# Projection units that hold half heads: two chunks a batch instead of four, and two groups of stacks read at the batch's head

## What is computed

```python
xn  = layernorm(x)
qkv = xn @ qkv_w + qkv_b                       # 512 -> 3 x 512, 32 heads of width D = 16
x1, x2 = split(q or k, 2, axis=-1)             # lower and upper 8 of a head's 16
q or k = concat([x1*cos - x2*sin, x2*cos + x1*sin])
ctx = softmax(causal(q @ k.T / sqrt(16))) @ v  # 32 heads, 512 x 512 scores
x = x + (ctx @ out_w + out_b) * silu(swiglu_ffn(xn))
x = x + block1_attn(layernorm(x)) * silu(block1_ffn(layernorm(x)))
```

## Time and profile before

| quantity | value |
|---|---|
| median of 3 runs | 650.18 us (648.63 to 650.63) |
| profiled execution, its own time | 646.0 us |
| span of the profile | 644.1 us |
| PE / DVE / ACT / POOL busy | 605.6 / 381.3 / 276.1 / 377.7 us |
| mean granted TensorE clock | 0.999 |
| batch 0: PE starts its first unit, slot 0 | 15.12, 40.07 us |
| batch 1: PE starts its first unit, slot 0 | 235.22, 259.79 us |

### The profile page before, as it was taken

The page is one execution under the profiler, slowest core; times in us unless marked ns, Lnnn a source line. Parts: engine busy times, 40 slices in busy tenths (PEclk is TensorE's granted clock), DMA queues, the critical chain, the costliest instruction groups (busy, mean ns, idle before and its releaser), DMA issues.

```text
span 644.1 us, 9815 instructions
## 1 busy us (share of the span) xinstructions
PE 605.6 (94%) x3348; PEld 417.9 (65%) x3348; DVE 381.3 (59%) x918; ACT 276.1 (43%) x439; POOL 377.7 (59%) x596
## 2 busy tenths in 40 slices
PE   2997999999999999889999999999999999999996
PEld 2865565666557888555556665687887566757564
DVE  4958768666426495786775663466975261515275
ACT  3524555555643633255554556355122343222323
POOL 4876656555334578676565553447989474921254
PEclk9999999999999999999999999999999999999999
DMA  8778865753422327568477644824600000000012
GB/s 284 221 224 280 248 177 146 209 135 92 98 99 67 99 82 214 171 187 243 134 220 226 177 104 117 319 81 172 204 26 1 0 1 2 0 1 0 2 50 82
DMA packets 60225, 83.63 MB, mean 130 GB/s; under 512 B 17920, under 2 KB 26496, under 8 KB 60176
## 3 DMA queue, kind: packets, MB, share of 16 engines
q1 hardware_dynamic: 57392, 73.84, 38.9%
q10 hardware_dynamic: 2784, 9.18, 4.0%
HBM read 65.17 MB, written 26.99 MB: 143 GB/s over the span
## 4 chain that ended last, share of the span: by engine, by line
PE 75%; DVE 8%; POOL 5%; DMA 5%; issue 3%; SPq 2%; ACT 2%; DVEq 0%; ACTq 0%; POOLq 0%
PE proj_ps L922 9%; PE ctx_ps L1080 6%; PE proj_ps L923 6%; PE proj_ps L924 6%; PE score_ps L952 5%; PE proj_ps L1128 3%; PE scoreT_ps L961 3%; PE score_ps L922 3%; PE proj_ps L1129 3%; PE score_ps L924 2%; PE score_ps L923 2%; PE scoreT_ps L922 2%; PE scoreT_ps L924 2%; PE scoreT_ps L923 2%; POOL w_lo L741 2%
## 5 line engine op out<-in xcount | busy, mean ns | idle before, releaser
L741 POOL TENSOR_TENSOR w_lo<-raw,w_hi 128x512 fp32r<-128x512 f32 x98 | 132.7, 1359 | 67.8 <-ACT w_hi L1272 61.2
L1447 DVE CUSTOM_DVE_ANT_0 score_ps<-score_ps,causal 128x512 f32<-128x512 f32 (+3 forms) x256 | 120.0, 517 | 58.0 <-PE score_ps L952 57.6
L1316 ACT ACTIVATE probs_T<-scoreT_ps 128x1024 f32<-128x1024 f32 (+1 forms) x96 | 84.9, 884 | 80.9 <-PE scoreT_ps L961 80.1
L922 PE MATMUL proj_ps<-xn_hi,w_hi 128*128 128x512 f32 x224 | 99.5, 444 | 0.3 <-POOL w_lo L741 0.3
L923 PE MATMUL proj_ps<-xn_hi,w_lo 128*128 128x512 f32 x224 | 88.1, 393 | 0.0
L924 PE MATMUL proj_ps<-xn_lo,w_hi 128*128 128x512 f32 x224 | 87.8, 392 | 0.0
L739 POOL TENSOR_SCALAR w_hi<-raw 128x512 fp32r<-128x512 f32 x50 | 31.2, 625 | 49.4 <-PE proj_ps L924 48.5
L897 POOL TENSOR_TENSOR hsL<-hidden_T,hsH 128x256 fp32r<-128x256 f32 x44 | 38.2, 884 | 36.1 <-ACT hsH L1399 35.8
L922 PEld LDWEIGHTS proj_ps<-xn_hi,w_hi 128*128 128x128 f32 x224 | 41.9, 187 | 24.5 <-issue 9.5
L775 POOL TENSOR_SCALAR_AFFINE_SELECT probs_T<-probs_T 128x256 f32<-128x256 f32 x128 | 50.6, 416 | 10.9 <-ACT probs_T L1316 10.9
L952 PE MATMUL score_ps<-k_st,q_st 50*128 50x512 f32 (+3 forms) x256 | 44.4, 383 | 13.0 <-DVE row_max L1447 8.8
(11 more groups left out here) (303 smaller groups left out, 1307.9 us busy)
## 6 DMA issues: line engine op xcount, KB each, us to landing
raw<-w SPq DMA_DIRECT2D x98, 256.0 KB, 2.8
rows<-rows_hi SPq DMA_DIRECT2D x32, 256.0 KB, 3.8
arranged<-tern SPq DMA_DIRECT2D x96, 85.0 KB
q_st<-rows SPq DMA_DIRECT2D x32, 200.0 KB
k_st<-rows SPq DMA_DIRECT2D x32, 200.0 KB
rows<-rows_lo SPq DMA_DIRECT2D x16, 256.0 KB, 4.4
gate_w<-arranged ACTq DMA_DIRECT2D x4, 704.0 KB, 7.0
up_w<-arranged ACTq DMA_DIRECT2D x4, 704.0 KB, 7.8
```

The source lines that it names most:

```text
L741: nc.gpsimd.tensor_tensor(w_lo[n % SPLIT][:, :], raw[n % RAW][:, :], F32(w_hi[n % SPLIT][:, :]), ALU.subtract).then_inc(unit_ready, 1)
L922: nc.tensor.matmul(acc, lh, rh, start=first, stop=False)
L1316: nc.scalar.activation(probs_T[gp % 4][:, c:c + 2 * w].rearrange("p (h c) -> p h c", h=2), scoreT_ps[:, :, 0:w], ACT.Exp, scale=0.25).then ...
L1447: m = nc.vector.tensor_tensor_reduce(out=block, in0=block, in1=causal[:, S - w:], scale=1.0, scalar=-3e38, op0=ALU.add, op1=ALU.max, accum ...
```

## The change

A query or key unit now holds only the lower or only the upper 8 dimensions of 16 heads, so there are two chunks of 16 heads a batch, of four units each: query lower, query upper, key lower, key upper (`QK_UNIT`). `rope_first` needs two instructions of 128 partitions, `by_cos` and `by_sin`, and `rope_second` combines the cosine part of one half with the sine part of the other: lower = cos(lower) - sin(upper), upper = cos(upper) + sin(lower). So the sum of either half waits until both halves have been projected (`upper`, `turned_in`). The doubled tiles are now one for lower and one for upper.

The first chunk's four units stand at the head: FILL = 8, V is units 4 to 7, and two units (8 and 9) are run before slot 0 instead of three; 96 triples instead of 100 are dealt to the 53 slots. The second chunk's are units 9, 11, 13 and 15. `read_rows` of groups 0 and 1 both stand at the head, and the ternary weights are written among the loads of slot 0. The number of units, matmuls, splits, writes and reads is the same; DVE has 16 instructions fewer. The small theta matmul of batch 0 moves to another bank, and in batch 1 PE's wait for `combined` stands before unit 2 instead of before V.

```diff
-Q_UNIT, K_UNIT, V_UNIT = (0, 9, 12, 18), (1, 10, 13, 19), 2
-FFN_UNIT = [6, 7, 8, 11, 14, 15, 16, 17] + list(range(20, 34))
-IN_FRONT = 3 * KC
-FILL = 6
+QK_UNIT, V_UNIT = ((0, 1, 2, 3), (9, 11, 13, 15)), 4
+FFN_UNIT = [8, 10, 12, 14] + list(range(16, 34))
+CHUNKS = 2
+IN_FRONT = 2 * KC
+FILL = 8
 TRIPLES = (U_DOWN - FILL) * KC
 JOBS = U_DOWN - KC
-QK_OF = {**{u: (0, c) for c, u in enumerate(Q_UNIT)}, **{u: (1, c) for c, u in enumerate(K_UNIT)}}
+QK_OF = {u: (c, n // 2, n % 2) for c in range(CHUNKS) for n, u in enumerate(QK_UNIT[c])}
...
+def upper(u):
+    c, t, _ = QK_OF[u]
+    return QK_UNIT[c][2 * t + 1]
+
+
+def turned_in(s):
+    return [u for u in sorted(QK_OF) if u >= FILL and unit_slot(upper(u)) + 2 + QK_OF[u][2] == s]
+
+
 def rest_in_slot(s):
-    return [u for u in sorted(QK_OF) if u >= FILL and unit_slot(u) + 3 == s]
+    return turned_in(s - 1)
 
 
 def written_in(s):
-    return [u for u in sorted(QK_OF) if u >= FILL and unit_slot(u) + 4 == s]
+    return turned_in(s - 2)
 
 
 def read_in(s):
-    return next((g for g in range(1, GROUPS) if (1 if g == 1 else max(6 * g - 6, unit_slot(K_UNIT[g // 2]) + 6)) == s), None)
+    return next((g for g in range(2, GROUPS) if max(6 * g - 6, unit_slot(QK_UNIT[g // 4][3]) + 7) == s), None)
 
 
 def down_in(s):
@@ -178,8 +189,8 @@
...
-HI_BY_ACT = FILL + 3
-RAW_HEAD = 12
+HI_BY_ACT = FILL + 1
+RAW_HEAD = 13
...
     def rope_job(b, u):
-        return 8 * b + 2 * QK_OF[u][1] + QK_OF[u][0]
-
-    def written(b, t, c, x):
-        return rows_d[b][t][c][:, 2 + D * x:2 + D * x + D, :].rearrange("h d s -> d h s")
+        c, t, h = QK_OF[u]
+        return 8 * b + 4 * c + 2 * t + h
+
+    def written(b, t, c, h, x):
+        first = 2 + D * x + D // 2 * h
+        return rows_d[b][t][c][:, first:first + D // 2, :].rearrange("h d s -> d h s")
...
                 n = GROUPS * b + g
-                c, h = g // 2, 4 * (g % 2)
-                sp.wait_ge(rows_stored, 96 * (KC * b + c + 1))
+                c, h = g // 4, 4 * (g % 4)
...
-                    if u == 9:
-                        write_rows(b, Q_UNIT[0])
-                        write_rows(b, K_UNIT[0])
+                    if u in (10, 11):
+                        write_rows(b, QK_UNIT[0][u - 10])
+                    if u == 12:
+                        write_rows(b, QK_UNIT[0][2])
+                        write_rows(b, QK_UNIT[0][3])
                 read_rows(b, 0)
+                read_rows(b, 1)
                 for s in range(SCORE_SLOTS + 1):
-                    if b == 0 and s == 1:
-                        for w in range(3):
-                            sp.wait_ge(wp_ready, w + 1)
-                            for x, src in enumerate((tern_pos[w], tern_neg[w])):
-                                sp.dma_start(tern_d[w][x].rearrange("(p n) -> p n", p=P), F32(src[:, :])).then_inc(tern_stored, 16)
                     for u in written_in(s):
                         write_rows(b, u)
                     if read_in(s) is not None:
                         read_rows(b, read_in(s))
-                    for u in raw_in_slot(s):
+                    for x, u in enumerate(raw_in_slot(s)):
                         load(b, u)
+                        if b == 0 and s == 0 and 1 <= x <= 3:
+                            sp.wait_ge(wp_ready, x)
+                            for half, src in enumerate((tern_pos[x - 1], tern_neg[x - 1])):
+                                sp.dma_start(tern_d[x - 1][half].rearrange("(p n) -> p n", p=P), F32(src[:, :])).then_inc(tern_stored, 16)
                     if b == 0 and s == 3:
                         write_edges(1)
                     for x in range(copies_in(b, s)):
...
+                    if b and u == 5:
+                        pool.wait_ge(out_used, KC * b)
+                        nc.gpsimd.memset(V[:, :, :].rearrange("p t (h c) -> p t h c", c=32)[:, :, :, D:], 1.0).then_inc(ones_set, 1)
                     split(u0 + u)
                     if b == 0 and u == 1:
                         nc.gpsimd.memset(F32(max_cols[:, :, :, :]), 0.0).then_inc(cols_set, 1)
-                if b:
-                    pool.wait_ge(out_used, KC * b)
-                    nc.gpsimd.memset(V[:, :, :].rearrange("p t (h c) -> p t h c", c=32)[:, :, :, D:], 1.0).then_inc(ones_set, 1)
-                rope_lo(b, Q_UNIT[0])
-                rope_lo(b, K_UNIT[0])
+                    if u in (5, 6):
+                        rope_lo(b, QK_UNIT[0][u - 5])
+                rope_lo(b, QK_UNIT[0][2])
+                rope_lo(b, QK_UNIT[0][3])
                 for s in range(SCORE_SLOTS + 2):
                     if max_in(s) is not None:
                         join_maxima(b, max_in(s))
...
-                for u in (Q_UNIT[0], K_UNIT[0]):
+                for u in QK_UNIT[0]:
+                    if b and job(u) == 2:
+                        pe.wait_ge(combined, 2 * NT * (b - 1) + NT)
                     for kc in range(KC):
                         if u == 0:
                             n0 = norm_use(b, kc)
@@ -1008,9 +1026,7 @@
                 if b == 0:
                     pe.wait_ge(ones_set, 2)
                     pe.wait_ge(asum_ready, 3)
-                    nc.tensor.matmul(proj_ps[1][:, 0:3], V[:, 0, 0:P], abs_sums[:, :], start=True, stop=True).then_inc(tot_ready, 1)
-                else:
-                    pe.wait_ge(combined, 2 * NT * (b - 1) + NT)
+                    nc.tensor.matmul(first_ps[0][:, 0:3], V[:, 0, 0:P], abs_sums[:, :], start=True, stop=True).then_inc(tot_ready, 1)
                 for kc in range(KC):
...
-                for u in range(5 if b else RAW, FILL):
+                for u in range(5 if b else RAW, HI_BY_ACT):
                     split_hi(UNITS * b + u)
-                rope_hi(b, Q_UNIT[0])
-                split_hi(UNITS * b + FILL)
-                rope_hi(b, K_UNIT[0])
-                for u in range(FILL + 1, HI_BY_ACT):
-                    split_hi(UNITS * b + u)
+                    if u in (5, 6):
+                        rope_hi(b, QK_UNIT[0][u - 5])
+                rope_hi(b, QK_UNIT[0][2])
+                rope_hi(b, QK_UNIT[0][3])
                 act.wait_ge(ones_set, 2 + b)
...
             def rope_first(b, u):
 
-                (t, c), r = QK_OF[u], rope_job(b, u)
-                ps, bias = job_bank(u), qk_bias[:, 4 * t + c:4 * t + c + 1]
+                h, r = QK_OF[u][2], rope_job(b, u)
+                ps, bias = job_bank(u), qk_bias[:, r % 8:r % 8 + 1]
                 dve.wait_ge(proj_done, JOBS * b + job(u) + 1)
                 if r >= 2:
-                    dve.wait_ge(turned_ready, r - 1)
-                nc.vector.scalar_tensor_tensor(out=by_cos[t][:, :], in0=ps[:, :], scalar=bias, in1=rope_cos[:, :],
+                    dve.wait_ge(turned_ready, r - h)
+                nc.vector.scalar_tensor_tensor(out=by_cos[h][:, :], in0=ps[:, :], scalar=bias, in1=rope_cos[:, :],
                                                op0=ALU.add, op1=ALU.mult).then_inc(cos_ready, 1)
-                nc.vector.scalar_tensor_tensor(out=by_sin[t][0:64, :], in0=ps[64:128, :], scalar=bias[64:128], in1=rope_sin[64:128, :],
-                                               op0=ALU.add, op1=ALU.mult).then_inc(sin_half, 1)
-                nc.vector.scalar_tensor_tensor(out=by_sin[t][64:128, :], in0=ps[0:64, :], scalar=bias[0:64], in1=rope_sin[0:64, :],
+                nc.vector.scalar_tensor_tensor(out=by_sin[h][:, :], in0=ps[:, :], scalar=bias, in1=rope_sin[:, :],
                                                op0=ALU.add, op1=ALU.mult).then_inc(proj_free, 1)
 
             def rope_second(b, u):
 
-                (t, c), r = QK_OF[u], rope_job(b, u)
+                h, r = QK_OF[u][2], rope_job(b, u)
                 dve.wait_ge(cos_ready, r + 1)
-                dve.wait_ge(sin_half, r + 1)
-                dve.wait_ge(*released(b, u))
+                dve.wait_ge(*released(b, upper(u)))
                 if r >= 2:
                     dve.wait_ge(rows_lo_ready, r - 1)
-                nc.vector.tensor_tensor(turned_rows[t][:, :], by_cos[t][:, :], by_sin[t][:, :], ALU.add).then_inc(turned_ready, 1)
+                nc.vector.tensor_tensor(turned_rows[h][:, :], by_cos[h][:, :], by_sin[1 - h][:, :],
+                                        (ALU.subtract, ALU.add)[h]).then_inc(turned_ready, 1)
 
             def first_ropes(b):
 
-                for u in (Q_UNIT[0], K_UNIT[0]):
-                    rope_first(b, u)
-                    rope_second(b, u)
+                for t in range(2):
+                    for u in QK_UNIT[0][2 * t:2 * t + 2]:
+                        rope_first(b, u)
+                    for u in QK_UNIT[0][2 * t:2 * t + 2]:
+                        rope_second(b, u)
 
             norm_stats(0)
             norm_rows(0)
...
-                    for u in units_after(s - 1):
-                        if u in QK_OF:
-                            rope_second(b, u)
+                    for u in turned_in(s):
```

(3 more changed lines are left out.)

37 lines of the change are left out of this document (19 added, 18 removed).

## The result

| | before | after |
|---|---|---|
| median of the runs, us | 649.46 (648.63 to 650.63, 4 runs) | 686.76 (685.26 to 688.83, 4 runs) |
| profiled execution: span / own time, us | 644.1 / 646.0 | 684.6 / 686.58 |
| PE busy / DVE busy, us | 605.6 / 381.3 | 614.9 / 366.3 |

The changed kernel takes 1.0607 times the time of the one before (95% interval 1.0579 to 1.0634): slower, as forecast, but by 37 us and not by 11, and outside the range. (The two medians of the table alone stand at 1.0574 to 1; by either figure the slowdown is several times the noise.)

The account below looks back on a forecast made before the run. PE was taken as the bound, busy 605.6 of 644.1 us. Heads +12.3 and +12.6, moved units -2 x 2.73 and slots -8.0 give +11.4 on 646.0, or 657.4; with the runs' 4.2 offset 661.6 us, range 652 to 671.

Parts of the forecast that it names:

- The heads: From each batch's first unit to slot 0: slot 0 comes 12.3 us later in batch 0, 12.6 in batch 1.
- A write of `rows_hi` lands 3.8 us after its issue: Both write rounds of each head: landing taken as 3.9 us, bounds 2.8 and 4.9.
- Here SP has nothing else under way: Last read before slot 0: lands 4.4 us after issue, between 2.8 and 6.07, with no other transfers beside it.
- Together -8.0: Slot phases: half the row-maxima waits, 4.4 us, and both late stack reads, 3.6, go; bounds -3.6 and -15.9.
- -5.5 for the moved units: Slot phases: four triples fewer in each batch save PE 2.73 us per phase, taken whole.
- the loads from 13 on start at about 50: Raw loads behind the head's reads, needed in slot 6: cost put at nothing.
- The relief of DVE: Slots: each rotation loses a 0.76 us instruction, 12 us over 16 units; PE's row-maxima waits shrink by 4.4 us.
- Rival 2: Slots paced by DVE gain more than the heads lose, closing all 15.9 us of gaps: -4.1, 646 us; chance 0.07.
- both stalls in each head: PE waits 2.5 us before unit 8 and 7.4 us before slot 0, as given for batch 0.
- Rival 1: Heads: only one write-and-read round trip counts, slot 0 at 46.2 and 266.1; sum -1.1, 649 us; chance 0.09.
- rival 5: Heads: writes and read land after 2.8 us, 3.8 less a head; sum +3.8, 654 us; chance 0.08.
- Rival 3: Heads: slower transfers or a clock fallen behind the stalls cost about 7.4 us more, 669 us; chance 0.13.

Follow-up runs that it names:

- Loads first: The changed kernel with 16 heads outermost, separate buffers and three units in front, plus slot 0's raw loads before group 1's read and ternary writes last: 652.6 us.
- heads outermost: The changed kernel with unit columns ordered head by head, so writes go as 16 heads by 8 by 512: 672.3 us, ratio 1.0349.
- the clock kept up: The changed kernel with 24 and 52 unused matmuls per batch in the two stalls of each head: 688.7 us, ratio 1.0612.
- warm start: The kernel before with 12 unused matmuls of 128 columns while PE waits for its input: 646.4 us, ratio 0.9984.

## Why the prediction was wrong

The sum was +11.4 and the profiled executions give +40.5 (spans of 684.6 and 644.1). The 29.1 between them, with -0.6 from an earlier first unit:

- **The heads, +22.0.** Forecast 37.3 and 37.2 us long (24.95 + 12.3, 24.57 + 12.6), measured 47.9 and 48.6. This is the step that failed: "A write of `rows_hi` lands 3.8 us after its issue; I take 3.9", taken for both rounds of writes of a head. The row was of writes with 16 outermost, and the change's own writes have 8; they landed in 6.5 and 7.0. In batch 0 the 10.0 us by which slot 0 comes later than 52.4 are: last write of job 1 issued 0.8 later; its landing 6.5 for 3.9, +2.6; from load 12 to job 3's last write 5.6 for 3.5, +2.1, as SP's own issues lengthen (3.21 for two writes); landing 7.0 for 3.9, +3.1; reads from the first issue to slot 0 6.95 for 5.5, +1.4. With 16 outermost the two landings measured 4.2 and 3.8, near the forecast, and the 5.6 became 4.3; the reads stayed at 6.8. So the reads were a second term sized too low, by 1.4 a head, whatever the pattern: "Here SP has nothing else under way" left out that group 1's reads go out right behind them. Whether those slow them wasn't settled, since with loads in their place ("Loads first") it is no shorter: the first read goes out at 42.10 and slot 0 starts at 49.67. The pattern's price, from the kernel with the heads outermost, is 14.5 us in the median and 15.0 of the heads' 22.0. The bounds of 2.8 to 4.9 were taken from rows of the old pattern, so the range could not hold it.
- **The slots, +7.6.** "Together -8.0", and -5.5 for the moved units, came out as -5.9. PE's idle time in the two stretches behind the heads fell by 2.9 and 1.4 us (8.8 to 5.9, 18.2 to 16.8), not by 8.0. Row maxima gave 3.6 (of 4.4) and the two late reads 3.6 as forecast, but the wait for `max_cols` took 3.5 of it. The prediction's "the loads from 13 on start at about 50, needed in slot 6" priced this at nothing, and it was false: they start at 58.6, and POOL's first joined maxima stand behind their splits. PE's busy time there fell by 0.4 and 1.1, not 2.73 each. Part of it is the clock behind each stall; how much wasn't settled, but it is little: with the clock kept up PE's busy time there fell by 1.2 and 0.8, and that kernel was no faster.
- **The relief of DVE** came out near its size: alone it is worth 4.1 us, against the 4.4 taken. That is in part luck: the row maxima fell by 7.0 and not by half of 8.8, and 3.0 came back in other waits. DVE's busy time fell by 15.0 in the change, not by 12. Rival 2, the faster side, had nothing in it: even with the pattern mended the stretches behind the heads are only 4.2 us shorter than before, not 19.5.
- **The offset, -4.0.** The runs' median stood 4.2 above the profiled execution before; after, 0.2. So +29.1 - 4.0 is, to the rounding, the miss of 25.2 (686.8 less 661.6).

Right were the direction, the mechanism (both stalls in each head, in these places and with these releasers), and no wait for `k_st` at slot 6. The two signs named for a wrong forecast (slot 0 before 47, PE's idle time in the slots down by over 10) both pointed to the faster side, and neither came. Rival 1, one round trip alone, is refuted by ACT's 12.01 us wait; so is rival 5. Rival 3 named costlier stalls with a price of 7.4: right in kind, a third in size. Even with the pattern mended the change is 3.5% slower, of which the shared buffers are the next 11 us (672.3 less 661.4).

**The clock.** The prediction held the trace against the rule of "TensorE: Matmul & The Clock Gate" in the Trainium skill, in its part on the clock gate, that an idle PE falls to half rate. That was a misreading, of a column that reads 1.00 in either case. The transposes right behind the 10.7 us wait start 0.21 us apart in the kernel before, and 0.11 in the one with a warm start. In order of time, PE's first matmuls of before, and the first after PE was kept busy:

```profile
10.94 0.42 PE L998 MATMUL proj_ps<-ident,xn_first 128*128 128x128 f32 x1
11.15 0.42 PE L998 MATMUL scoreT_ps<-ident,xn_first 128*128 128x128 f32 x1
```

```profile
10.32 0.27 PE L1001 MATMUL proj_ps<-ident,xn_first 128*128 128x128 f32 x1
10.43 0.27 PE L1001 MATMUL scoreT_ps<-ident,xn_first 128*128 128x128 f32 x1
```

So the trace agrees with the page's rule here, and its price is small: slot 0 of the changed kernel starts with matmuls of 0.79 in place of 0.50 (2.4 GHz to 1.2) behind its waits of 11.7 and 10.6 us, and keeping the clock up bought nothing in the time.
